# Three preparatory programs of a fused attention and memory kernel joined into one, with the context products set between transposes

## What is computed

```
K        = ctx @ Wk.T + bk                         # 256 x 2048
scores   = (ln(x) @ Wq.T + bq) @ K.T / sqrt(2048)  # per batch, 64 wide
x1       = x + tanh(g_xattn) * softmax(scores) @ ctx
h        = ln(x1)
query    = h @ fWq.T                               # 64 wide
router   = (query @ Wr.T) @ (aux_keys @ Wr.T).T / sqrt(48) + log_rel      # 512 slots
w        = softmax over the top 8 slots of query @ aux_keys.T / 8 + log_rel
aux      = (w @ aux_values) @ Wvd.T @ Wvu.T
u        = clip(0.5 * norm_var(h) + 2.5 * sigmoid(gelu(h @ Wu1.T + bu1) @ Wu2.T + bu2), 0, 5)
gate     = sigmoid(w1 * clip((u - 0.5) / 1.5, 0, 1) + b), zero below 0.05
out      = h + gate * aux, added to x1 with tanh(g_ffn)
```

## Time and profile before

| | us |
|---|---|
| runs | 1154.72, 1151.8, 1153.51 |
| median | 1153.51 |
| profiled execution, its own time | 1153.86 |
| its span in the profile | 1152.0 |
| busy: TensorE / VectorE / ScalarE / GpSimd | 1071.0 / 769.2 / 558.8 / 178.0 |
| mean granted TensorE clock | 0.966 |

### The profile page before, as it was taken

One profiled execution on the slowest core, in us unless ns is written; L12 is line 12 of the kernel. 1 busy time (PEld: TensorE's weight loads), 2 busy tenths in 40 slices (PEclk: granted clock), 3 DMA queues, 4 the chain that ended last, 5 costly groups with the idle time before them and its releaser, 6 DMA issues. The chain is left out here.

```text
span 1152.0 us, 19589 instructions
## 1 busy us (share of the span) xinstructions
PE 1071.0 (93%) x6890; PEld 1020.4 (89%) x6890; DVE 769.2 (67%) x1822; ACT 558.8 (49%) x870; POOL 178.0 (15%) x337
## 2 busy tenths in 40 slices
PE   6799989977796999999999999999999994899998
PEld 6799989976696999999999999999999994677876
DVE  6755545454413787768778787777777765688786
ACT  3233388647701555545454545545454544454553
POOL 0600000000000222222322222231322221000000
PEclk9999999988798999999999999999999996899999
DMA  7323546686533898374343745345643427699997
GB/s 269 134 109 138 201 173 253 257 268 211 152 74 96 209 240 209 98 209 109 111 120 98 192 118 144 92 127 153 155 112 107 133 86 246 248 364 422 423 426 315
DMA packets 101980, 218.89 MB, mean 190 GB/s; under 512 B 47540, under 2 KB 63956, under 8 KB 82904
## 3 DMA queue, kind: packets, MB, share of 16 engines
q1 hardware_dynamic: 96760, 180.68, 51.1%
q10 hardware_dynamic: 4608, 33.56, 7.0%
q0 software_dynamic: 576, 4.19, 0.9%
HBM read 174.10 MB, written 54.79 MB: 199 GB/s over the span
## 5 line engine op out<-in xcount | busy, mean ns | idle before, releaser
L55 PE MATMUL tk_hidden_sum<-b_weights,k_turned 128*128 128x384 f32 x512 | 176.3, 344 | 0.0
L56 PE MATMUL tk_hidden_sum<-b_weights,k_turned 128*128 128x384 f32 x512 | 173.2, 338 | 0.0
L57 PE MATMUL tk_hidden_sum<-b_weights,k_turned 128*128 128x384 f32 x512 | 173.1, 338 | 0.0
L55 PE MATMUL tk_b_sum<-b_weights,k_turned 128*128 128x320 f32 (+1 forms) x528 | 170.2, 322 | 2.5 <-DVE k_turned L1237 1.6
L57 PE MATMUL tk_b_sum<-b_weights,k_turned 128*128 128x320 f32 (+1 forms) x528 | 164.4, 311 | 0.0
L56 PE MATMUL tk_b_sum<-b_weights,k_turned 128*128 128x320 f32 (+1 forms) x528 | 164.4, 311 | 0.0
L1228 DVE STREAM_TRANSPOSE tk_bank<-k_rows 128x512 f32<-128x512 f32 x128 | 133.6, 1068 | 15.3 <-DMA k_rows<-in_x_dram 15.0
L1047 ACT ACTIVATE k_turned<-tk_bank 128x512 fp32r<-128x512 f32 x128 | 73.9, 595 | 103.6 <-DVE tk_bank L1228 86.4
L55 PEld LDWEIGHTS tk_b_sum<-b_weights,k_turned 128*128 128x128 f32 x528 | 100.1, 190 | 3.9 <-issue 3.7
L56 PEld LDWEIGHTS tk_b_sum<-b_weights,k_turned 128*128 128x128 f32 x528 | 100.1, 190 | 0.0
L57 PEld LDWEIGHTS tk_b_sum<-b_weights,k_turned 128*128 128x128 f32 x528 | 99.8, 189 | 0.0
(11 more groups left out here) (272 smaller groups left out, 2582.3 us busy)
## 6 DMA issues: line engine op xcount, KB each, us to landing
k_rows<-in_x_dram SPq DMA_DIRECT2D x48, 1024.0 KB, 4.9
k_rows<-in_x_dram SPq DMA_DIRECT2D x128, 256.0 KB, 5.1
k_rows<-in_Wk_dram SPq DMA_DIRECT2D x16, 1024.0 KB, 4.8
k_rows<-in_Wq_dram SPq DMA_DIRECT2D x16, 1024.0 KB, 4.9
late_x<-in_x_dram SPq DMA_DIRECT2D x16, 1024.0 KB, 12.9
out_dram<-k_rows ACTq DMA_DIRECT2D x16, 1024.0 KB, 9.8
out_dram<-late_x ACTq DMA_DIRECT2D x16, 1024.0 KB, 10.3
b_weights<-scratch_b SPq DMA_DIRECT2D x6, 1024.0 KB, 8.2
```

Of the source, the lines that this page charges most:

```text
L55: pe.matmul(out, lh, rh, start=start, stop=False, skip_group_check=skip)
L56: pe.matmul(out, lh, rl, start=False, stop=False, skip_group_check=skip)
L57: return pe.matmul(out, ll, rh, start=False, stop=stop, skip_group_check=skip)
```

## The change

One program per engine takes the place of the first three, so engines do not meet before the output.

- GpSimd's two passes become eight pieces each, of 512 elements.
- ScalarE makes Wq's first row sum ahead of the last high parts of the keys.
- The slot inputs are loaded behind the loads of the keys. bq's row product (in bank 4 now) and VectorE's copy of it go behind job 0 of the memory weights.
- The jobs have a new order: Wvd, two of aux_values, Wvu, two of aux_values, fWq, four of Wu1. The first batch's score weights are loaded behind job 7's load.
- The product of the context with itself takes 256 columns in place of 128 and stands between the transposes of jobs 0 to 3; the value products stand between those of jobs 4 and 7; the 192-column products between those of jobs 8 to 10; the 384-column ones follow.
- Centring: ScalarE sums, VectorE scales and subtracts (`centre`).
- In the first tile ScalarE's exponential and VectorE's attention stand ahead of tile 1's turning; tile 1's load stands ahead of the wait for the second context rows. VectorE scales the context with itself (`gram_scale`) apart from the 384 columns (`context_scale`).
- GpSimd's memset of `cw_low` has nothing ahead of it but the context's stores.

The diff, cut to its core:

```diff
@@ keys_stage: scalar
             for u in range(2):
                 parts_hi(2 * j + u + 1, 1 - u)
                 high_part(act, 2 * j + u, u)
+        first_sum(act)
         parts_hi(KC - 1, 1)
@@ score_weights_stage: gpsimd
-            pool.tensor_tensor(cent, f32(ctxT[0][:]), mean, ALU.subtract).then_inc(shifted, 1)
-            pool.wait_ge(shifted, 1)
-            pool.tensor_tensor(cent, cent, f32(ctxT[1][:]), ALU.add).then_inc(summed, 1)
+        for k in range(8):
+            own = slice(2 * k, 2 * k + 2)
+            pool.tensor_tensor(cent[:, own, :], f32(ctxT[0][:, own, :]), mean[:, own, :],
+                               ALU.subtract).then_inc(shifted, 1)
+        for k in range(8):
+            own = slice(2 * k, 2 * k + 2)
+            pool.wait_ge(shifted, k + 1)
+            pool.tensor_tensor(cent[:, own, :], cent[:, own, :], f32(ctxT[1][:, own, :]),
+                               ALU.add).then_inc(summed, 1)
@@ ffn_stage: sync
+        for n in range(FFN_RING, len(jobs)):
+            sp.wait_ge(turned, GROUPS * (n - FFN_RING + 1))
+            load_ffn(sp, io, rows, rows_in, n)
+            if n == QUERY + 1:
+                sp.wait_ge(keep["mt_out"], MT_STORED)
+                sp.wait_ge(keep["cent_out"], 16 * 4)
+                load_batch_b(sp, scr, keep, 0)
@@ ffn_stage: tensor
+        def turn(n, g):
+            if g == 0 and n >= QUERY:
+                pe.wait_ge(centred, n - QUERY + 1)
+            if g == 0 and n < QUERY:
+                pe.wait_ge(rows_in[ffn_buffer(n)], 16 * (n // FFN_RING + 1))
+            if n:
+                pe.wait_ge(lo_done, GROUPS * (n - 1) + g + 1)
+            else:
+                pe.wait_ge(out_lo, g + 1)
...
+        def gram(r, cols):
+            if cols[0] == 0:
+                pe.wait_ge(out_lo, (6, 8)[r])
+            for c in cols:
+                split_product(pe, ps_gram[r][:, 0:CR], context(r, c), tuple(cT[i][:, c, :] for i in range(2)),
+                              c == 0, c == KC - 1, True)
...
+        for g in range(GROUPS):
+            turn(0, g)
+            gram(0, (2 * g, 2 * g + 1))
+        keys["tensor_row"](pe)
+        for g in range(GROUPS):
+            turn(1, g)
+            gram(0, (8 + 2 * g, 9 + 2 * g))
...
+        for g in range(GROUPS):
+            value_products(0, g)
+            turn(4, g)
...
+        for g in range(GROUPS):
+            turn(5, g)
+        turn_values(0)
...
+        for g in range(GROUPS):
+            turn(6, g)
+        for g in range(GROUPS):
+            value_products(1, g)
+            turn(7, g)
+        for g in range(GROUPS):
+            query_part(3 * g, 3 * g + 3)
+            turn(8, g)
+        turn_values(1)
...
+        for r in range(2):
+            for g in range(GROUPS):
+                hidden_part(r, g)
@@ ffn_stage: scalar
+        def sum_rows(n):
...
+            act.wait_ge(rows_in[ffn_buffer(n)], 16 * (n // FFN_RING + 1))
+            act.activation(mine, mine, ACT.Copy, accum_out=own["sums"][0:r, n:n + 1]).then_inc(row_summed, 1)
...
+        for n, (r, dst) in enumerate(jobs):
+            if QUERY <= n + 1 <= LAST:
+                sum_rows(n + 1)
@@ ffn_stage: vector
+        def centre(n):
...
+            dve.wait_ge(row_summed, n - QUERY + 1)
+            dve.tensor_scalar(nmean, own["sums"][0:r, n:n + 1], -1.0 / D, None, ALU.mult)
+            dve.drain()
+            dve.tensor_scalar(mine, mine, nmean, None, ALU.add).then_inc(centred, 1)
...
+        for n, (r, dst) in enumerate(jobs):
+            if QUERY <= n + 1 <= LAST:
+                centre(n + 1)
@@ prepare_and_token_block: sync
             for r in range(2):
+                if r == 1:
+                    load_tile(sp, 1)
                 sp.wait_ge(S["cw_low"], r + 1)
@@ prepare_and_token_block: scalar, tile
+                if first:
+                    soft(t)
                 if not last:
                     x_hi(t + 1, 1 - u, 0)
                     x_hi(t + 1, 1 - u, 1)
-                soft(t)
+                if not first:
+                    soft(t)
```

More of the change, by code:

```diff
@@ L308, in vector_row @@
         dve.wait_ge(row_done, 1)
[L309 removed]
+        return dve.tensor_scalar(keep["bq_rows"][:].rearrange("p b n -> p (b n)"), ps_row,
                           ATT_SCALE, None, ALU.mult)
@@ L1089, in squares, with tile @@
                                accum_out=rsq[u][:]).then_inc(S["squares"], 1)
-            def tile(t, u, late=True, late_z_too=True, last=False):
+            def tile(t, u, late=True, late_z_too=True, last=False, first=False):
                 if late_z_too:
@@ L1116, in context_hi @@
                 act.activation(cw_hi[r], cw[r], ACT.Copy).then_inc(S["cw_high"], 1)
+            weights["scalar"](act)
+            ffn_scalar(act)
             row_sum(0, 0)
@@ L1120, in _ @@
             context_hi(0)
-            act.wait_ge(S["cw_product"], 2)
+            act.wait_ge(keep["cw_product"], 2)
             for g in range(G):
@@ L1124, in _ @@
             context_hi(1)
-            tile(0, 0, late=False, late_z_too=False)
+            tile(0, 0, late=False, late_z_too=False, first=True)
             tile(1, 1, late_z_too=False)
@@ L1398, in tile @@
                 soft_scores(t, u, j // 4)
+                if not (last or first):
+                    turn_x(t + 1, 2)
+                soft_att(t, u, first or second)
                 if first:
@@ L1402, in tile @@
                     turn_x(t + 1, 1)
-                elif not last:
-                    turn_x(t + 1, 2)
-                soft_att(t, u, first or second)
                 if late_z_too:
@@ L1644, in gated_cross_attention_and_memory @@
             keep[n] = [m.sem(f"{n}{i}") for i in range(count)]
+        keep["slots"] = slots_memory(keep)
+        stages, outer_banks = Memory(nc, outer, "st"), ExitStack()
+        keep["banks"] = [Memory(nc, outer_banks, "tk").ps(f"bank{i}") for i in range(8)]
         with ExitStack() as first:
@@ L1655, in gated_cross_attention_and_memory @@
             keep["wq_sum"], keep["wq_nmean"] = m.sb("wq_sum", [P, KC]), m.sb("wq_nmean", [P, KC])
-            score_weights_block(nc, io, scr, keep)
+            for n in ("key_product", "key_biased", "mu_done"):
+                keep[n] = stages.sem(n)
+            keys = keys_stage(nc, io, scr, keep, Memory(nc, outer, "ky"), m)
+            weights = score_weights_stage(nc, io, scr, keep, Memory(nc, outer, "sw"), keys)
         with ExitStack() as second:
@@ L1680, in gated_cross_attention_and_memory @@
                 keep["bu1"], keep["wu2"] = m.sb("bu1", [P, HU]), m.sb("wu2", [P, HU])
-                ffn_block(nc, io, scr, keep)
-                token_block(nc, io, scr, keep)
+                prepare_and_token_block(nc, io, scr, keep, keys, weights)
+            outer_banks.close()
             output_block(nc, io, scr, keep)
```

737 lines of the change are left out of this document (374 added, 363 removed).

## The result

The changed kernel takes 1106.37 us (median of four runs, 1104.87 to 1107.39) against 1153.03 (four runs, 1151.80 to 1154.72): a ratio of 0.958, 95% interval 0.9565 to 0.9596. The profiled execution has a span of 1103.7 us at a mean granted clock of 0.985, against 1152.0 at 0.966. The prediction was 1108.6 in a range of 1101 to 1122.

A forecast was written before the change was run, and what follows sets the result against it. TensorE, busy 93% of the span, bounds the kernel, so only its idle and low clock can give time. Gains 8.6 + 1.5 + 29.0 + 7.3 = 46.4, less 1.5: 1153.86 - 44.9 = 1109.0, against the median 1108.6; range 1101 to 1122.

The forecast's parts named there:

- Part 1: Keys: GpSimd's passes in pieces shorten VectorE's wait and remove TensorE's 7.0 us idle and half-clock restart; gain 8.6 us, bounds 0 to 8.6.
- rival of a lock that holds across pieces: Keys: nothing lets VectorE in between GpSimd's pieces, so L261 and L218 wait as before; price 8.6 us, 1117.2, chance 0.13.
- DVE writes low parts four groups (5.6 us) ahead of PE: Keys: VectorE's lead over TensorE, said to hide a wait of 1.1 us twice per block of keys.
- slow return: TensorE's low clock after an idle: 0.9 and 0.6 us priced in the keys, 2.5 us (0 to 6) in the memory weights.
- Part 2: Start of the score weights: first row sum made earlier, TensorE idle 1.6 us instead of 3.1; gain 1.5, bounds 0 and 3.1.
- Part 3: Memory weights without block borders, context products between transposes: 80.4 us instead of 109.4; gain 29.0, bounds 18 and 36.
- VectorE's centring: Memory weights: new in-place subtraction of 2048 on VectorE, taken as 1.4 us with its mean, bounds 0.9 and 2.35.
- rival of a stage bound by ScalarE and VectorE: Memory weights: centred jobs cost TensorE 2.5 us more each and the clock stays low; 15 us more, 1123.6, chance 0.14.
- rival of SP's queue: Memory weights: b loads share the queue with jobs 8 to 10 and x tile 0; 48 us late, 1156.6, chance 0.02.
- Part 4: First token tile: exponential first and tile 1's load earlier, tile 1 starts at E+22.2 against E+29.5; gain 7.3, bounds 5.5 and 10.
- the low clock after it stays: First token tile: after TensorE's 1.58 us wait for the first turned x, the low clock was expected to remain as before.
- The 1.5 us taken off for small unseen waits: Whole sum: 1.5 us subtracted from the 46.4 us gain because a stage rewritten like this will have small unseen waits.

## Why the prediction was right

The predicted gain was 44.9 us, 46.7 were measured between the medians, and each of the four parts came out near where it was put.

- **Part 1, 8.6 predicted, 9.1 to 9.4 measured.** The mechanism is the one given. VectorE's L218 took 1.5, 4.8 and 9.1 us with pieces of 512, 2048 and 4096 elements, so the exclusion of VectorE and GpSimd holds for an instruction, and ends between two that follow each other. (By the Trainium skill, SBUF — State Buffer, section SBUF: two separate sides, it lasts for a whole instruction. These three runs agree.) The rival of a lock that holds across pieces falls: in the changed kernel L262 and L218 were both through 1.1 us before the end of the first pass, whose pieces have no wait between them, and in the two-piece run L218 did not last to the end of the second. One step failed: "DVE writes low parts four groups (5.6 us) ahead of PE". It was counted from the order of the code, and its two figures do not fit each other: a group is 16 instructions of 0.1174, 1.88 us, so 5.6 us is three groups. The two-piece run and the kernel before give 3.67 us each, so the trace of before had it already: 10.68 us late, 7.01 us of idle. With eight pieces, 1.6 us late, either lead was enough, so the error did not reach the sum. The term was 0.5 to 0.8 us short. Part of that is the slow return, for which 1.6 was allowed beside 7.0 of idle. The 76 instructions missing in the kernel before are 8.9 us, so 1.9 of them are the return, and in the run with whole passes it lasted longer still. What is left, some 0.2 us in the kernel before, was not located.
- **Part 2, 1.5 predicted, 1.55 measured,** idle 1.54 for a predicted 1.6.
- **Part 3, 80.4 us predicted, 80.28 measured.** The sum is closer than its terms, and that is luck: what was too much in waits and clock, 2.8, and what was too little in work, 2.7, cancel. Waits came to 3.0 instead of 5: the first transposes of job 6 1.20 us where 2.3 was laid out behind job 5, the second value products 0.36 for 0.7, the query products 1.41 for 1.3, job 7 none for 0.8. VectorE's centring, bounded between 0.9 and 2.35 and taken as 1.4 with its mean, is 1.28 + 0.15. The slow return is 1.7 us (six microseconds at 0.72) for 2.5. TensorE's own work was put too low by about 2.7 us: 80.28 - 3.0 - 1.7 = 75.6 against 72.9. By the distances between the starts of matmuls in the profile after, the 256-wide products took some 24.6 (priced 23.0, with 0.4 of the difference for the width), the 192- and 384-wide ones 28.4 (27.4), the small products 4.0 (3), and the transposes 18.6 (19.5). As an estimate by cause: 6.1 and 2.2 (the border's slow return in the run with a border), 3.1 for the wait on the memset, 17.1 for the products between transposes, less 1.2 for the width, is 27.3 of the 29.2. The rest would be the split centring, the order of the jobs and the value products between transposes (in the run with the products apart they stayed there), none of which was tried alone.
- **The rival of a stage bound by ScalarE and VectorE** falls for this kernel: 75.9 of 80 us busy. The run with the products apart shows what that rival looks like, 97.4 us at a granted 0.89. There its mechanism holds.
- **The rival of SP's queue** showed nothing: TensorE has no wait on a DMA from T0 to E. It did wait once for aux_values, 2.8 us, when the products stood apart and it asked for job 1 sooner.
- **Part 4, 7.3 predicted, 7.9 measured.** Load asked for at E+4.3 (predicted E+4.4), tile 1 turned from E+11.8 (E+12.8), tile 1's first matmul at E+21.55 (E+22.2). The idle is 3.18 instead of 2.5, for a reason that was missed: "the low clock after it stays" was wrong. 315 to 320 us runs at 1.00, where the same wait of 1.58 before was followed by 0.57 for four microseconds, so TensorE was through with tile 0 at E+17.3 instead of E+19, and waited for a chain that it does not set. The split between the two edits was not predicted, and the runs give it: 6.2 us to the load's place, 1.1 to the exponential's; at L1042, where the whole tile has gained 7.3 (E+33.46 before, E+26.19 after), 6.5 and 0.4.
- **The 1.5 us taken off for small unseen waits** was not needed. With it left out the forecast would have been 1107.1.

## What to carry to other kernels

A long elementwise GpSimd pass beside a busy VectorE is cheap to cut into pieces (here a pass took 10.4 us instead of 9.0 for it): what counts is that one piece is shorter than VectorE's lead, and that lead is best read from a stall in the trace, as how late the engine was less how long the next one idled. Matmuls that need nothing from the slower engines belong between transposes that wait for them: of what this gave, somewhat over half was waiting and the rest the clock. When a wait at the head of a chain is removed, look for what the consumer needs next; here the copy came 3.8 us earlier and half of one was gained.

## What the runs showed of the hardware

- The clock's answer to one wait is no constant. A wait of 1.58 us was followed by four microseconds at 0.57 in the kernel before and by full clock after; two waits of 2.48 and 1.90 us cost nothing where one of 3.18 left 0.66 over the five microseconds behind it; in six other runs with that one wait, of 3.06 to 3.44 us, it was 0.66 to 0.69, and 0.50 in the run with the products apart, after 3.20; 2.83 us in the keys cost nothing; the same 7.01 us was followed by some 3.6 us at half clock in the kernel before (59 to 61 us already at 0.66) and by 4.9 in the run with whole passes (58.5 to 63 at 0.50, 63 to 65 at 0.91). After the same 8.89 us in the output the fall lasted differently from one execution to the next.
- From E to the end, the same code took 791.3 us (the run with the border) to 797.6 (the run with the products apart) in the profiles of eight kernels. Gains of 2 us in one stage can be read in the timeline and not in one time of the whole.
- A 128 x 2048 subtraction in place on VectorE with one SBUF input takes 1.28 us, a little over half of the 2.35 us of one with two.
